# The join of the two alignment halves interleaved with the last choice operations, and the value projections ahead of the weights' sums on TensorE

## The reference, cut to what matters

```python
x = x + tanh(g_xattn[0]) * align(ctx, layernorm(x))          # dynamic time warping
x = x + tanh(g_ffn[0])   * ffn(layernorm(x), w1, conv, w2)   # ternary weights
x = x + tanh(g_xattn[1]) * attention(layernorm(x), ctx, Wq, Wk, Wv, Wo, biases)
x = x + tanh(g_ffn[1])   * patterns(layernorm(x), ...)       # three top-k stages

def align(small, large):             # per sequence: context rows against tokens
    D = sqrt(max(|a|^2 + |b|^2 - 2 a.b, 0))                  # 375 x 112
    R[i, j] = D[i, j] + min(R[i-1, j], R[i, j-1], R[i-1, j-1])
    # backtrack from the last cell: at each cell argmin of (diagonal, up, left)
    # every context row on the path is added to the token that it is aligned with
```

## Time and profile before

| what | value |
|---|---|
| runs of the kernel before | 594.98, 596.68, 597.45 us (median 596.68) |
| span of the profiled execution | 594.4 us; its time outside the span is not shown |
| mean granted TensorE clock | 0.856 of full speed |
| busy: TensorE, VectorE, ScalarE, GpSimdE | 73%, 71%, 46%, 14% of the span |
| chain that ended last, by engine | TensorE 55%, VectorE 25%, ScalarE 10%, issue 5%, GpSimdE 4% |
| forward wavefront, VectorE (line 976) | starts 58.7 to 108.3 us |
| backward walk, VectorE (line 1049) | starts 119.3 to 169.9 us |

### The profile page before, as it was taken

One profiled execution on the slowest core, in us unless ns is written; L12 is line 12 of the kernel. 1 busy time (PEld: TensorE's weight loads), 2 busy tenths in 40 slices (PEclk: granted clock), 3 DMA queues, 4 the chain that ended last, 5 costly groups with the idle time before them and its releaser, 6 DMA issues.

```text
span 594.4 us, 10573 instructions
## 1 busy us (share of the span) xinstructions
PE 433.4 (73%) x3584; PEld 294.6 (50%) x3584; DVE 424.1 (71%) x1719; ACT 273.5 (46%) x657; POOL 81.7 (14%) x233
## 2 busy tenths in 40 slices
PE   2799699742268899578999999999999664602106
PEld 2468586521146555445677776776455553202103
DVE  7644999899946678978888888864444566275673
ACT  3754544732231644345465556654533553253440
POOL 6791000000032253704000000000000000000000
PEclk9998699855559799999999999999999898855556
DMA  9700003288004977310056958600300272000002
GB/s 278 211 1 2 1 1 117 93 148 169 19 1 132 130 144 160 103 40 0 3 80 97 203 81 147 183 1 2 142 0 2 78 276 72 1 0 1 1 1 62
DMA packets 34666, 47.25 MB, mean 79 GB/s; under 512 B 5541, under 2 KB 32054, under 8 KB 32822
## 3 DMA queue, kind: packets, MB, share of 16 engines
q1 hardware_dynamic: 34614, 46.58, 33.2%
HBM read 37.87 MB, written 8.60 MB: 78 GB/s over the span
## 4 chain that ended last, share of the span: by engine, by line
PE 55%; DVE 25%; ACT 10%; issue 5%; POOL 4%; DVEq 0%; POOLq 0%; ACTq 0%
PE ps L2194 8%; PE ps L2148 4%; DVE PR L1049 4%; PE ps L2135 4%; ACT below L1769 4%; PE ps L2124 4%; PE ps L1916 4%; PE ps L2034 4%; PE ps L1924 3%; PE ps L2110 3%; PE ps L2322 2%; PE ps L1980 2%; DVE prod L1045 2%; DVE below L1395 2%; PE ps L1875 2%
## 5 line engine op out<-in xcount | busy, mean ns | idle before, releaser
L1263 DVE TENSOR_REDUCE negm<-ps 112x1 f32<-112x375 f32 x128 | 65.5, 543 | 9.2 <-PE ps L2124 6.0
L1740 ACT ACTIVATE E<-ps 125x448 f32<-125x448 f32 x96 | 52.0, 543 | 43.0 <-PE ps L2135 42.7
L2295 PE MATMUL ps<-cnt,same 128*128 128x3 bf16 (+4 forms) x40 | 6.9, 172 | 61.6 <-ACT below L1769 41.1
L2124 PE MATMUL ps<-ks,qs 96*112 96x375 bf16 x128 | 42.9, 345 | 1.7 <-DVE negm L1263 0.8
L2148 PE MATMUL ps<-E,v 125*32 125x112 f32 x768 | 42.1, 270 | 0.0
L1251 DVE TENSOR_REDUCE acts<-gel 128x4 f32<-128x448 f32 x32 | 19.8, 621 | 29.3 <-ACT gel L1708 29.1
L2135 PE MATMUL ps<-qs,ks 99*125 99x112 bf16 x384 | 39.2, 224 | 1.2 <-DVE qs L1284 0.7
L2135 PEld LDWEIGHTS ps<-qs,ks 99*125 99x125 bf16 x384 | 33.8, 137 | 9.7 <-issue 6.2
L2295 PEld LDWEIGHTS ps<-cnt,same 128*128 128x128 bf16 (+1 forms) x40 | 4.4, 110 | 65.1 <-issue 65.1
L1708 ACT ACTIVATE gel<-ps 128x448 f32<-128x448 f32 x32 | 17.3, 543 | 29.3 <-PE ps L2194 29.3
L789 POOL CAST kp<-kx 128x750 bf16<-128x750 f32 x8 | 7.1, 884 | 165.7 <-ACT path L1623 125.8
(11 more groups left out here) (388 smaller groups left out, 1117.9 us busy)
## 6 DMA issues: line engine op xcount, KB each, us to landing
ks<-key_parts SPq DMA_DIRECT2D x48, 187.5 KB, 7.0
piw<-fn_process_input_weights SPq DMA_DIRECT2D x8, 1024.0 KB, 4.9
key_parts<-kp SPq DMA_DIRECT2D x48, 93.8 KB
ctx_again<-in_ctx SPq DMA_DIRECT2D x7, 512.0 KB
keys<-kx SPq DMA_DIRECT2D x16, 187.5 KB, 2.1
kx<-keys SPq DMA_DIRECT2D x8, 375.0 KB, 6.8
ctxP<-in_ctx SPq DMA_DIRECT2D x8, 256.0 KB, 6.3
patn<-in_L_ffn_input_patterns SPq DMA_DIRECT2D x1, 2048.0 KB, 15.6
```

The costliest lines, as they stand in the source:

```text
L1263: drain(dve.tensor_reduce(negm[:, n:n + 1], bank(nm)[0:S, 0:SC], AX.X, ALU.max, negate=True), nm)
L1740: drain(fn(E[:, (KCH * f + c) % 6, :], bank(nm)[0:KC, 0:4 * S], ACT.Exp), nm)
L2124: fill(mm(bank(nm)[0:S, 0:SC], qs[0:SR, u // 4 % 3, n, :], ks[0:SR, u // 4 % 3, n, :], start=True, stop=True), nm)
```

## The change

There are five edits. In `plan_psum` and on TensorE the 24 value projections come before `wsum` and `bo`, right behind the weight transposes; TensorE waits there for the drain of the third weight (wvT). On ScalarE the drains of `V` come right behind the drains of the weights; the sum over w1 is put behind the drains of the third sequence and the sum over w2 behind those of the sixth, and the Tanh and the drain of `bo` follow the last. On VectorE the two operations on `wsum` move from step 16 to step 42. Two new single-column tiles, `own_least` and `own_entry`, are allocated. And what is left of the generator at the end of the wavefront, with the two clears and the two shuffles behind it, becomes one generator (`remaining`) whose pieces `meanwhile` issues between the operations of the join. The rows of the least value are now picked in each block by the block's own least (`own_least`), and after the minimum over blocks a new operation keeps a block's entry only where its own least is the least of all; a copy of one column is new too. Waits for everything issued so far (`settle()`) become waits for one named instruction (`settle(done)`).

```diff
@@ -113,11 +113,11 @@
         ring(("dwave", m))
     for w in range(4):
         ring(("attnWT", w))
-    ring("wsum")
-    ring("bo")
     for b in range(B):
         for c in range(KCH):
             ring(("V", b, c))
+    ring("wsum")
+    ring("bo")
     for u in range(2 * B):
         p.add(("kT", u), u % 4)
     p.add("joinF", 4)
@@ -360,6 +360,8 @@
         least = scratch.take("least", [128, 1])
         other = scratch.take("other", [128, 1])
         entry = scratch.take("entry", [128, 1])
+        own_least = scratch.take("own_least", [128, 1])
+        own_entry = scratch.take("own_entry", [128, 1])
         assert scratch.at <= last_stack + 2 * NH * SC
 
         rf = Region(c0)
@@ -985,52 +987,70 @@
                                        ALU.min, ALU.add).then_inc(wave, 1)
                 next(chooser)
                 dve.wait_ge(wave, t + 1)
-                if t == 16:
+                if t == 42:
 
                     wait_filled(dve, "wsum")
                     drain(ts(wmean[:, :], bank("wsum")[:, 0:2], 1.0 / (HID * D), 1e-5, ALU.mult, ALU.max), "wsum")
                     wait_drained(dve, "wsum")
                     dve.reciprocal(winv[:, :], wmean[:, :]).then_inc(winv_ready, 1)
             complete[0] = T
-            for _ in chooser:
-                pass
-
-
-            settle()
-            did(dve.memset(LG[:, T - 1, 0:1], 0.0))
-            did(dve.memset(UU[:, T - 1, 0:1], 0.0))
-            did(dve.stream_shuffle(LG[:, 0:T - 1, 0], LG[:, 1:T, 2 * RB], below_lane))
-            did(dve.stream_shuffle(UU[:, 0:T - 1, 0], UU[:, 1:T, 2 * RB], below_lane))
-
+
+            def remaining():
+                yield from chooser
+                settle()
+                did(dve.memset(LG[:, T - 1, 0:1], 0.0))
+                did(dve.memset(UU[:, T - 1, 0:1], 0.0))
+                did(dve.stream_shuffle(LG[:, 0:T - 1, 0], LG[:, 1:T, 2 * RB], below_lane))
+                yield
+                did(dve.stream_shuffle(UU[:, 0:T - 1, 0], UU[:, 1:T, 2 * RB], below_lane))
+
+            rest = remaining()
+
+            def meanwhile(n=1):
+
+                for _ in range(n):
+                    next(rest, None)
+
+            meanwhile(3)
             wait_filled(dve, "joinF")
             drain(dve.tensor_copy(meetF[:, :], bank("joinF")[:, 0:RB + 1]), "joinF")
+            meanwhile()
             wait_drained(dve, "joinF")
-            did(tt(cross[:, :], meetF[:, 0:RB], meetF[:, 1:RB + 1], ALU.min))
-            settle()
+            done = did(tt(cross[:, :], meetF[:, 0:RB], meetF[:, 1:RB + 1], ALU.min))
+            did(tt(hand(LG[0:64, T, 2 * RB:2 * RB + 1], [[-2, RB]]), meetF[0:64, 0:RB], meetF[0:64, 1:RB + 1],
+                   ALU.is_le))
+            settle(done)
             wait_filled(dve, "joinG")
             drain(tt(total[:, :], cross[:, :], hand(bank("joinG")[:, RB:RB + 1], [[-1, RB]]), ALU.add), "joinG")
-            did(tt(hand(LG[0:64, T, 2 * RB:2 * RB + 1], [[-2, RB]]), meetF[0:64, 0:RB], meetF[0:64, 1:RB + 1],
-                   ALU.is_le))
-            wait_drained(dve, "joinG")
-
-            def over_blocks(v, op):
-
-                for step in (1, 2, 4):
-                    settle()
-                    did(dve.stream_shuffle(other[:, :], v[:, :], [p ^ step for p in range(32)]))
-                    settle()
-                    did(tt(v[:, :], v[:, :], other[:, :], op))
-
-            did(dve.tensor_reduce(least[:, :], total[:, :], AX.X, ALU.min))
             did(tt(hand(LG[0:64, T, 2 * RB - 1:2 * RB], [[-2, RB]]), meetF[0:64, 0:RB], meetF[0:64, 1:RB + 1],
                    ALU.is_gt))
-            over_blocks(least, ALU.min)
-            settle()
-            did(stt(which[:, :], total[:, :], least[:, 0:1], row_id[:, :], ALU.is_le, ALU.mult))
+            wait_drained(dve, "joinG")
+
+            def over_blocks(v, op, done, between):
+
+                for step in (1, 2, 4):
+                    settle(done)
+                    done = did(dve.stream_shuffle(other[:, :], v[:, :], [p ^ step for p in range(32)]))
+                    between()
+                    settle(done)
+                    done = did(tt(v[:, :], v[:, :], other[:, :], op))
+                    between()
+                return done
+
+            done = did(dve.tensor_reduce(own_least[:, :], total[:, :], AX.X, ALU.min))
+            meanwhile()
+            settle(done)
+            did(dve.tensor_copy(least[:, :], own_least[:, :]))
+            done = did(stt(which[:, :], total[:, :], own_least[:, 0:1], row_id[:, :], ALU.is_le, ALU.mult))
             did(dve.stream_shuffle(LG[:, T, 0:1], LG[:, T, 2 * RB:2 * RB + 1], below_lane))
-            settle()
-            did(dve.tensor_reduce(entry[:, :], which[:, :], AX.X, ALU.max))
-            over_blocks(entry, ALU.max)
+            settle(done)
+            did(dve.tensor_reduce(own_entry[:, :], which[:, :], AX.X, ALU.max))
+            done = over_blocks(least, ALU.min, done, meanwhile)
+            settle(done)
+            done = did(stt(entry[:, :], own_least[:, :], least[:, 0:1], own_entry[:, :], ALU.is_le, ALU.mult))
+            done = over_blocks(entry, ALU.max, done, meanwhile)
+            for _ in rest:
+                pass
             settle()
 
             did(ts(hand(PR[0:64, T, 2 * RB + 1:2 * RB + 2], [[-2, RB]]), row_id[0:64, :], entry[0:64, 0:1], None,
@@ -1570,14 +1590,6 @@
                 nm = ("attnWT", i)
                 wait_filled(act, nm)
                 drain(fn(dst[:, :, :].rearrange("p h d -> p (h d)"), bank(nm)[:, :], ACT.Copy), nm)
-            act.wait_ge(loaded["ffnW"], 32)
-            did(fn(tern[0][:, :], w1n[:, :], ACT.Abs, accum_out=wabs[:, 0:1]))
-            fn(tern[1][:, :], w2n[:, :], ACT.Abs, accum_out=wabs[:, 1:2]).then_inc(wabs_ready, 1)
-            act.wait_ge(loaded["small"], 80)
-            fn(tg[:, :], gates[:, :], ACT.Tanh).then_inc(tg_ready, 1)
-            wait_filled(act, "bo")
-            act.wait_ge(tg_ready, 1)
-            drain(fn(gbo[:, :], bank("bo")[0:S, 0:D], ACT.Identity, scale=tg[0:S, 1:2]), "bo")
             act.wait_ge(ones_v_ready, KCH)
             for b in range(B):
                 for c in range(KCH):
@@ -1585,6 +1597,17 @@
                     wait_filled(act, nm)
                     drain(fn(v1[:, c, b, 0:NH * (HD + 1)].rearrange("p (h e) -> p h e", e=HD + 1)[:, :, 0:HD],
                              bank(nm)[0:KC, 0:D].rearrange("p (h e) -> p h e", e=HD), ACT.Copy), nm)
+                if b == 2:
+                    act.wait_ge(loaded["ffnW"], 32)
+                    did(fn(tern[0][:, :], w1n[:, :], ACT.Abs, accum_out=wabs[:, 0:1]))
+                if b == 5:
+                    fn(tern[1][:, :], w2n[:, :], ACT.Abs, accum_out=wabs[:, 1:2]).then_inc(wabs_ready, 1)
+                    settle()
+            act.wait_ge(loaded["small"], 80)
+            fn(tg[:, :], gates[:, :], ACT.Tanh).then_inc(tg_ready, 1)
+            wait_filled(act, "bo")
+            act.wait_ge(tg_ready, 1)
+            drain(fn(gbo[:, :], bank("bo")[0:S, 0:D], ACT.Identity, scale=tg[0:S, 1:2]), "bo")
             act.wait_ge(loaded["biasT"], 48)
             for u in range(2 * B):
                 nm = ("kT", u)
@@ -1896,6 +1919,15 @@
                         ins = tr(bank(nm)[:, D * h + 128 * c:D * h + 128 * c + 128],
                                  wnat[:, i, c, 128 * h:128 * h + 128], ident[:, :])
                 fill(ins, nm)
+            wait_drained(pe, ("attnWT", 2))
+            for b in range(B):
+                for c in range(KCH):
+                    nm = ("V", b, c)
+                    claim(pe, nm)
+                    for h in range(DH):
+                        ins = mm(bank(nm)[0:KC, 0:D], ctxT[:, h, b, KC * c:KC * c + KC], wvT[:, h, :],
+                                 start=(h == 0), stop=(h == DH - 1))
+                    fill(ins, nm)
             claim(pe, "wsum")
             pe.wait_ge(wabs_ready, 1)
             fill(mm(bank("wsum")[:, 0:2], ones[:, :], wabs[:, :], start=True, stop=True), "wsum")
@@ -1908,14 +1940,6 @@
                 ins = mm(bank("bo")[0:S, 0:D], bvT[:, h:h + 1].broadcast_to([128, S]), woT[:, h, :], start=False,
                          stop=(h == DH - 1))
             fill(ins, "bo")
-            for b in range(B):
-                for c in range(KCH):
-                    nm = ("V", b, c)
-                    claim(pe, nm)
-                    for h in range(DH):
-                        ins = mm(bank(nm)[0:KC, 0:D], ctxT[:, h, b, KC * c:KC * c + KC], wvT[:, h, :],
-                                 start=(h == 0), stop=(h == DH - 1))
-                    fill(ins, nm)
             for u in range(2 * B):
                 nm = ("kT", u)
                 t, b = u // B, u % B
```

## The result

Over 20 runs each the kernel after takes 593.39 us (587.93 to 599.67) against 596.16 (593.26 to 600.6) before. The ratio is 0.9946, 95% interval [0.9925, 0.9968]: 3.2 us less, between 1.9 and 4.5. The ratio leaves out two executions of after as slow (597.86 and 599.67, over 1.5% above its quickest); the medians of all twenty differ by 2.8. The profiled execution of after is the quickest of its 20 runs (587.93, span 586.2), so its span of 8.2 us less than before's 594.4 must not be read as the gain.

The account below looks back on a forecast made before the run. The chain of waits was taken to hang on when VectorE's backward walk starts. Terms 1.75, 2.35 and 2.2 sum to 6.3 from 110.13, a gain of 2.5, taken as 2.0: 596.68 − 2.0 = 594.7 us, range 592.6 to 596.8.

Parts of the forecast that it names:

- rival C: Behind the walk: shifted stages may meet their clock rises better or worse by about a us; 592.6 to 593.5, chance 0.14.
- Value projections first: On TensorE: projections start at 60.24 instead of 68.45 and end at 84.2, keys at 106.2; the join's 1.32 us wait goes.
- the loss of 3.25 at half clock: On TensorE: time the value projections lose, half a us for each of 6.5 us at half clock after their start.
- The 6.5 us from first matmul to the rise: On TensorE: delay from matmuls beginning again at 64.80 to the clock rise at about 71.3, assumed the same after the change.
- ScalarE's cover: On ScalarE: sums between value drains don't stop TensorE, and Tanh and bo's drain are covered; failing that, at most about 2 us.
- Step 42: On VectorE in the forward recurrence: wsum's two operations stand at about 92.4 without a wait, wsum being there at about 85.
- VectorE's tail: On VectorE from 110.13 to the walk: interleaved pieces sum to 6.3, walk starts at 116.4 instead of 118.94, gain 2.5.
- second and third: Tail pieces: join's copy to first shuffle, 1.75 (1.71 to 2.24); minimum's three rounds with six fillers, 2.35 (2.11 to 3.26).
- fourth: Last tail piece: new one-column operation (0.19 to 0.27), the maximum's three rounds (1.15) and the last 0.80; 2.2 in all.
- From one execution to the runs: Whole kernel: the profiled gain of 2.5 is cut to 2.0, between 2.5 and 1.2, as the idle time may be smaller.
- A: VectorE's tail: no operations overlap, only the idle time goes; gain 0 to 1.1, 595.6 to 596.7, chance 0.21.
- B: TensorE: clock stays low in the value projections, so slower; at half clock throughout some 39 us, 636; chance 0.05.

## Why the prediction was right

The time (594.7 forecast, 593.39 measured) lies in the range, and the sign and the cause are as forecast. The time alone can't show the cause: it lies in the forecast's own range (593.1 to 596.3) and in rival C's (592.6 to 593.5). The place in the trace does. Step by step:

- *Value projections first.* Right in place (60.08), wrong in size: the loss of 3.25 at half clock was 0.3 to 1.2 in eleven traces of this order. The 6.5 us from first matmul to the rise did not carry over, because TensorE now goes from transposes to projections without the pause: in five of the eleven the clock had risen before 60, when TensorE had run only transposes since 50.6, and in the others by 62.2. The projections end at 81.0 instead of 84.2, the keys at 103.0 instead of 106.2, outside the 104.5 to 106.5 that was given as a sign. It cost nothing: the scans set the join then, as the text said.
- *ScalarE's cover* held: drains kept up after three tiles. *Step 42*: the two operations stand at 92.80 (92.4 forecast), without a wait.
- *VectorE's tail.* Forecast 1.75, 2.35 and 2.2; measured 111.82 − 110.20 = 1.62, 113.83 − 111.82 = 2.01 and 116.15 − 113.83 = 2.32. The overlap was as said, but no term stayed between its ends. The text's second and third passed their lower ends (1.71 and 2.11), its fourth its upper end (2.22), since the new operation on one column took 0.37 (113.83 to 114.20) and not 0.19 to 0.27. The 2.11 was no lower end: it counts the last shuffle to its end, while the next operation of the chain is issued 0.30 before that shuffle ends (113.83 against 113.55 + 0.58). The fillers themselves took 114.13 − 111.89 = 2.24, no less than before. These errors partly cancel, and the gain of 2.79 is at the upper end that was given. The experiment without overlap shows that it hangs on the overlap.
- *From one execution to the runs.* The discount rested on the idle time varying; the repeat shows 0.54 against 1.32, and the walk's gain against the two profiles of before is 2.8 and 2.1. The base was a little high: the median of twenty runs of before is 596.16, not 596.68. And the span of 594.4 was not that of a quick execution: in every run on record the time is 1.7 above the span, so that profile stands for about 596.1. The plain medians give a gain of 2.8, the column at equal clock 595.3 − 593.2 = 2.1. The runs scatter too much (2 to 3 us each), and the correction is too doubtful, to tell these apart. By the text's own threshold 593.39 is faster (below 593.7), to which it gave 0.30.
- *Rivals.* A is disproved by the experiment. B did not occur: in no trace of this order did the projections last over 22 (at half clock they would take 41). C's sign can't be told: behind the walk one execution of after was 5.4 ahead of before's profile, another 4.2 behind (595.8 − 594.4 + 2.76).

The Trainium skill, "VectorE: DVE Perf Modes", section "The DRAIN you can't avoid", gives a measurement in which waits between operations cost nothing extra. Here they did cost: 9.76 against 5.95. The same section adds that a next operation that is not held starts earlier, which the prediction left out; the operations that overlap in the rows agree with that.

What exactly moves the clock's rises behind the walk stays open. Of the 5.4 us, 1.9 arise between 229 and 256 in before's time, where the clock is full in both, so the clock isn't all of it.

## What to carry to other kernels

When a short stretch waits for another engine and then runs a chain of dependent small operations, take both away together: in this kernel interleaving gained nothing as long as the other engine arrived late (3.66 us of waiting), and the earlier arrival gained only half without it. Put independent work between dependent VectorE operations, with a wait for the named instruction and not for all. And judge a gain of half a per cent at the place in the trace where it arises: it repeated within 0.03 us there, while whole runs scattered by 12.

## What the runs showed that I had not expected

- The clock rose while TensorE had run only transposes (0.61 in the stretch from 59 to 60 of after). In the repeat of before it rose there too, fell to half in the pause and rose again at 70.1; in before's first profile it had not risen when the pause began, and rose at 71.3 only. And 3.94 us of idle matmuls ahead of the expansion did not raise it in the profiled execution.
- One and the same operation on 112 x 8 numbers (line 1188 before, 1208 after) took 1.47 to 1.48 in twelve of the fourteen profiles, 0.70 in the first of after and 0.23 in that of the idle matmuls in the gap, with TensorE's clock full. The traces point at GpSimdE. In thirteen of them an operation of GpSimdE was running when it began, and it ended 0.02 to 0.04 behind that one: at 243.71 behind 243.68 in before, at 238.32 behind 238.30 in after. In the profile with 0.23 none was running. No run tried it without GpSimdE's work. Before, then after:

```profile
242.12 1.56 POOL L795 TENSOR_TENSOR kp<-kx,kp 128x750 bf16<-128x750 f32 x1
242.23 1.48 DVE L1188 TENSOR_SCALAR sx<-sx,tg 112x8 f32<-112x8 f32 x1
```

```profile
237.49 0.81 POOL L795 CAST kp<-kx 128x750 bf16<-128x750 f32 x1
237.62 0.70 DVE L1208 TENSOR_SCALAR sx<-sx,tg 112x8 f32<-112x8 f32 x1
```
